# Four transposed-row loads, issued from ScalarE's queue instead of SyncE's, in a two-layer graph network kernel

## The chip, the cores and the metric

The kernel runs on one core of one Trainium2 chip. The metric is the time of one execution on the device in microseconds. Other times below are from one profiled execution; the profile counts them from the start of its span.

## What is computed

For each of 128 graphs of 128 nodes with 384 features, two layers of a directed graph network run, then a residual and a layer norm. The reference, cut to what matters:

```python
def layer(h, params):
    wl, b_l, ws, b_s, wr, b_r, g, beta = params
    u = jnp.einsum('bid,bjd->bij', h, h) / temper
    a = jax.nn.softmax(u, axis=-1)
    delta = a * adjacency_matrix
    attn = delta / (jnp.sum(delta, axis=-1, keepdims=True) + 1e-10)
    hl = h @ wl.T + b_l
    hs = h @ ws.T + b_s
    hr = h @ wr.T + b_r
    diag_a = jnp.diagonal(attn, axis1=1, axis2=2)
    ctx = (jnp.einsum('bij,bjd->bid', attn * upper, hl) + diag_a[..., None] * hs
           + jnp.einsum('bij,bjd->bid', attn * lower, hr))
    o = (ctx - mean) / jnp.sqrt(var + LN_EPS) * g + beta
    return (jax.nn.relu(o), None)
x = _layernorm(x + _L0_gnn_ref(x, adj, ...), axis=-1)
```

## The kernel before

One iteration `i` of a software pipeline works on several graphs at once: the projections of layer 1 for graph `i`, those of layer 2 for graph `i-3`, scores for graphs `i+1` (layer 1) and `i-2` (layer 2), the gathers (attention times projections) of graph `i-4` (layer 2) and `i` (layer 1). Layer 1 is `k = 0` in the code and layer 2 is `k = 1`. The function `run` issues the iterations: 0 to 7 written out, 8 to 123 in a hardware loop unrolled by four, and the rest, to 132, written out. Every engine has its own program with its instructions in an order written by hand, and semaphores join the programs. There is no planner.

Values are split into a rounded high part (ScalarE) and a low rest (GpSimd or VectorE), so that TensorE computes a product as three matmuls. TensorE's program is `project_and_score`, which interleaves 18 projection matmuls (L394) with three score steps (L388) and, after projection 14, one more score matmul that needs ScalarE's copy `cross` (L428), and `gather` (L458). The two layers share one set of accumulators `p_proj`, so a projection waits until VectorE has taken the former one out with its bias (`add_bias`, L562 and L566).

Two matrices are transposed through memory. The attention: VectorE transposes 32x32 blocks (L586), SyncE stores them (`store_attn`, L311) and loads them back block by block with four DMAs (`load_attn`, L328) into `attnT_whole`, which GpSimd cuts into its two sides (`cut_sides`, L816). The normalised rows of layer 1: ScalarE writes `normed` (L716), VectorE transposes its blocks (L596), SyncE stores them to `rows_mem` (`store_rows`, L333) and loads them back with four DMAs into `rowsT` (`load_rows`, L344). ScalarE then applies gain, shift and ReLU to `rowsT` in `relu_rows` (L733) in the iteration after the load and rounds the result (L739). `rowsT` has one buffer, so `load_rows` waits until `relu_rows` has read the graph before (`s_relu`), and until the store has landed (`s_rows_out`).

SyncE issues every DMA, in this order in an iteration: `xt_raw` (L355), the adjacency of layer 2 (L359), `store_rows`, `store_attn`, `xn` (L366), `load_rows`, `load_attn`, the adjacency of layer 1 (L373), `out` (L377). A store of the rows or of the attention waits for VectorE, and everything behind it in the queue waits with it.

ScalarE's order in an iteration is: `relu_rows(i-2)`, `cross_scores(0, i+1)` (L694), `high_sides(1)` (L707), the normalised rows (L716), `exponentials(0)` (L699), `high_sides(0)`, `high_projections(0)` (L712), `high_input` (L756), the squares (L744), the output rows (L716), `cross_scores(1, i-2)` (L694), `high_projections(1, i-3)` (L712), `exponentials(1, i-2)`. In iterations 0 and 1 the rounding of layer 2's weights (L760) ends the list.

Of the kernel before, what the change touches and what calls it, by code (L numbers as in the profile page):

```python
# [36 lines left out]
B = 32  # L37
# [15 lines left out]
def graph_block(nc: bass.Bass, xT: bass.AP, x: bass.AP, adj: bass.AP, WT: bass.AP, bias: bass.AP,  # L53
                gain_cols: bass.AP, shift_cols: bass.AP, gain_row: bass.AP, shift_row: bass.AP, out: bass.AP):
    G, N, D = x.shape
    C = D // P
# [6 lines left out]
    with ExitStack() as ctx:  # L63
        def sb(name, shape, dtype=F32):
            return ctx.enter_context(nc.sbuf_tensor(name, shape, dtype))
# [4 lines left out]
        def sem(name):  # L70
            return ctx.enter_context(nc.semaphore(name))
# [30 lines left out]
        rowsT = sb("rowsT", [P, C, N])  # L102
# [32 lines left out]
        rows_mem = [nc.dram_tensor(f"rows_mem_{slot}", (P, D), F32, kind="Internal").ap() for slot in range(2)]  # L135
# [16 lines left out]
        s_rows_out = [sem("s_rows_out_even"), sem("s_rows_out_odd")]  # L152
        s_rows_in = [sem("s_rows_in_even"), sem("s_rows_in_odd")]
# [43 lines left out]
        s_relu = sem("s_relu")  # L197
# [10 lines left out]
        def live(i, b):  # L208

            return not isinstance(i, int) or 0 <= b < G  # L210

        def done(eng, s, b):

            if not isinstance(b, int) or b >= 0:
                eng.wait_ge(s, b + 1)

        def moved(eng, pair, b, slot):

            if not isinstance(b, int) or b >= 0:
                eng.wait_ge(pair[slot], (b - slot) * 8 + 16)  # L220
# [11 lines left out]
        def direct_rows(i, b):  # L232

            return isinstance(i, int) and b == G - 1
# [40 lines left out]
        def col(tile, slot, k):  # L275
            return tile[:, slot, k:k + 1]
# [4 lines left out]
        def _(sp):  # L281
# [49 lines left out]
            def store_rows(b, slot):  # L331
                done(sp, s_rows_blocks, b)
                sp.dma_start(rows_mem[slot], rows_blocks[:]).then_inc(s_rows_out[slot], 16)  # L333

            def load_rows(b, slot):
                moves, read = (b - slot) * 8 + 16, b
                if not isinstance(b, int):
                    moves, read = sp.snap(moves), sp.snap(read)
                sp.wait_ge(s_rows_out[slot], moves)
                if not isinstance(b, int) or b >= 1:  # L340
                    sp.wait_ge(s_relu, read)
                blocks = rows_mem[slot].rearrange("(r a) (c s b) -> s a c r b", a=B, b=B, c=C)
                for s in range(4):
                    sp.dma_start(rowsT[s * B:(s + 1) * B, :, :].rearrange("a c (r b) -> a c r b", b=B),  # L344
                                 blocks[s]).then_inc(s_rows_in[slot], 16)

            done(sp, s_diag[0], 0)
            sp.dma_start(adj_tile[0][:, 0], adj[2]).then_inc(s_adj[0][0], 16)

            def iteration(i, p):  # L350
                q = 1 - p
                if live(i, i + 3):

                    done(sp, s_lo[0], i + 1)
                    sp.dma_start(xt_raw[:, q], xT[i + 3]).then_inc(s_xt[q], 16)  # L355
                if live(i, i - 1):

                    done(sp, s_attn[1], i - 3)
                    sp.dma_start(adj_tile[1][:, q], adj[i - 1]).then_inc(s_adj[1][q], 16)  # L359
                if live(i, i - 1) and not direct_rows(i, i - 1):  # L360
                    store_rows(i - 1, q)
                store_attn(i, p)
                if live(i, i - 3):

                    done(sp, s_y, i - 5)
                    sp.dma_start(xn[:, q], x[i - 3]).then_inc(s_xn[q], 16)  # L366
                if live(i, i - 1) and not direct_rows(i, i - 1):
                    load_rows(i - 1, q)
                load_attn(i, p)
                if live(i, i + 3):  # L370

                    done(sp, s_attn[0], i + 1)
                    sp.dma_start(adj_tile[0][:, q], adj[i + 3]).then_inc(s_adj[0][q], 16)  # L373
                if live(i, i - 5):

                    done(sp, s_o, i - 5)
                    sp.dma_start(out[i - 5], o[:, q]).then_inc(s_out[q], 16)  # L377

            run(sp, iteration)

            moved(sp, s_out, G - 2, 0)
# [308 lines left out]
        def _(act):  # L690
            def cross_scores(k, b):

                done(act, s_parts[k], b)
                nc.scalar.activation(cross[k][:], p_score[k][:, LO, :], ACT.Copy).then_inc(s_cross[k], 1)  # L694
# [20 lines left out]
            def normalise(which, rows_in, rows_out, s_rows):  # L715
                nc.scalar.activation(rows_out, rows_in, ACT.Identity, bias=nbias[:, which:which + 1],  # L716
                                     scale=rstd[:, which:which + 1]).then_inc(s_rows, 1)
# [23 lines left out]
            def squared_denominators(k, b, slot):  # L741
# [2 lines left out]
                nc.scalar.activation(eps_units[k][:, slot:slot + 1], col(rows[k], slot, EXPSUM), ACT.Square,  # L744
                                     bias=col(rows[k], slot, ADJSUM), scale=ATTN_EPS).then_inc(s_denom2[k], 1)

            def finish(i, q):
                moved(act, s_out, i - 7, q)
                done(act, s_y_nbias, i - 5)
                normalise(2, y[:], o[:, q, :], s_o)  # L750
# [19 lines left out]
            def iteration(i, p):  # L770
                q = 1 - p
                if isinstance(i, int) and i == 0:
                    high_input(1, 1)
                if live(i, i - 2):
                    relu_rows(i, i - 2, p)
                if live(i, i + 1):
                    cross_scores(0, i + 1)
                if live(i, i - 4):
                    high_sides(1, i - 4)
                if live(i, i - 1):  # L780
                    done(act, s_nbias, i - 1)
                    if not direct_rows(i, i - 1):

                        done(act, s_rows_blocks, i - 2)
                    normalise(0, gathered[:], normed[:], s_normed)
                if live(i, i + 1):
                    exponentials(0, i + 1, q)
                if live(i, i):
                    high_sides(0, i)
                    high_projections(0, i)  # L790
                if live(i, i + 2):
                    high_input(i + 2, p)
                if live(i, i + 1):
                    squared_denominators(0, i + 1, q)
                if live(i, i - 3):
                    squared_denominators(1, i - 3, q)
                if live(i, i - 5):
                    finish(i, q)
                if live(i, i - 2):
                    cross_scores(1, i - 2)  # L800
                if live(i, i - 3):
                    high_projections(1, i - 3)
                if live(i, i - 2):
                    exponentials(1, i - 2, p)
                if isinstance(i, int) and i == 0:
                    high_weights(1, UP)
                    high_weights(1, LOW)
                if isinstance(i, int) and i == 1:
                    high_weights(1, SELF)
# [118 lines left out]
```

## Time and profile before

| | before |
|---|---|
| median of 3 runs | 1686.35 us (1685.6 to 1686.82) |
| the profiled execution | 1685.81 us |
| its span in the profile | 1683.7 us |
| TensorE matmul busy | 1641.0 us (97%) |
| TensorE weight loads busy | 1590.4 us (94%) |
| VectorE busy | 1455.0 us (86%) |
| GpSimd busy | 1185.6 us (70%) |
| ScalarE busy | 933.2 us (55%) |
| share of 16 DMA engines | 42.5% |

The profiled execution lies 2.1 us over its span and 0.5 us under the median of the runs. Busy time counts no waits, no semaphore work and no issuing of DMAs; the rows of engine "SPq" are SyncE's queue and show how long an issue held it. A row of the timeline gives the start, the length, the engine, the line and the operation, and "x4" means that four like instructions were merged into it.

### The profile page before, as it was taken

Reading aid. Unit: us, or ns where it says so; the run is one execution under the profiler, and the core shown is the slowest. Engines: PE = TensorE matmul, PEld = TensorE weight load, DVE = VectorE, ACT = ScalarE, POOL = GpSimd, SP = SyncE. Lnnn points to the kernel's source line nnn. Section 1 sums busy time; section 2 is a strip of 40 time slices with the busy share of each in tenths; the row PEclk is TensorE's granted clock in tenths of the full one; section 3 lists DMA queues with packets and bytes.
Section 4 is the critical chain, followed back from the end, with each engine's and each line's share of the span. In section 5 each row is a group of like instructions: output and inputs, shape, how many; then the busy total and the mean of one; then the engine's idle time right before and its main releaser. Section 6 shows DMA issues by size and latency. Waiting matters only on the chain.

```text
span 1683.7 us, 35740 instructions
## 1 busy us (share of the span) xinstructions
PE 1641.0 (97%) x9478; PEld 1590.4 (94%) x9478; DVE 1455.0 (86%) x4625; ACT 933.2 (55%) x2438; POOL 1185.6 (70%) x1539
## 2 busy tenths in 40 slices
PE   6999999999999999999999999999999999999985
PEld 5999999999999999999999999999999999999985
DVE  6788888888888888888888888888888888888876
ACT  4555555555555555555655555555555555555552
POOL 3577777767767767767777777776776776777762
PEclk9999999999999999999999999999999999999997
DMA  5444444444444444444444444444444444444431
GB/s 183 93 110 107 108 108 107 110 106 107 113 104 111 112 104 110 112 104 111 109 107 109 110 108 108 105 112 107 107 113 104 111 111 104 110 112 105 107 84 36
DMA packets 471767, 180.88 MB, mean 107 GB/s; under 512 B 355776, under 2 KB 470720, under 8 KB 471744
## 3 DMA queue, kind: packets, MB, share of 16 engines
q1 hardware_dynamic: 471744, 180.61, 42.5%
q8 instruction: 9, 0.15, 0.0%
q14 instruction: 14, 0.11, 0.0%
HBM read 113.77 MB, written 66.72 MB: 107 GB/s over the span
## 4 chain that ended last, share of the span: by engine, by line
POOL 62%; issue 20%; DVE 8%; DMA 3%; ACT 3%; SPq 2%; PE 2%; POOLq 1%; DVEq 0%; ACTq 0%
POOL proj_split L252 24%; POOL rstd L825 11%; POOL attnT L816 10%; POOL attnT_split L821 10%; POOL hT_layer L850 5%; POOL nbias L829 3%; DVE proj L562 2%; ACT proj_split L712 2%; DMA rows_mem<-rows_blocks 1%; DVE p_gather L531 1%; SPq L344 1%; DVE y L537 1%; DVE stats L541 1%; PE p_proj L394 1%; DMA attnT_whole<-attn_mem 1%
## 5 line engine op out<-in xcount | busy, mean ns | idle before, releaser
L394 PE MATMUL p_proj<-w,hT_layer 128*128 128x384 f32 x6912 | 1397.8, 342 | 1.1 <-DVE proj L562 0.7
L394 PEld LDWEIGHTS p_proj<-w,hT_layer 128*128 128x128 f32 x6912 | 1168.8, 189 | 26.2 <-DVE proj L562 21.3
L252 POOL TENSOR_TENSOR proj_split<-proj,proj_split 128x768 fp32r<-128x768 f32 x252 | 465.6, 1848 | 409.3 <-ACT proj_split L712 409.2
L712 ACT ACTIVATE proj_split<-proj 128x768 fp32r<-128x768 f32 x256 | 214.8, 839 | 546.5 <-DVE proj L562 546.5
L458 PE MATMUL p_gather<-proj_split,attnT_split 128*128 128x384 f32 x1536 | 313.6, 339 | 21.2 <-POOL attnT_split L821 10.9
L458 PEld LDWEIGHTS p_gather<-proj_split,attnT_split 128*128 128x128 f32 x1536 | 272.8, 190 | 24.6 <-POOL attnT_split L821 18.1
L562 DVE TENSOR_TENSOR proj<-p_proj,bias_all 128x768 f32<-128x768 f32 x256 | 243.3, 950 | 5.6 <-PE p_proj L394 5.1
L825 POOL TENSOR_TENSOR rstd<-veps,neg_half 128x1 f32<-128x1 f32 x384 | 211.9, 552 | 33.9 <-DVE veps L510 15.0
L388 PE MATMUL p_score<-hT_layer 128*128 128x256 f32 x768 | 217.2, 284 | 8.1 <-POOL hT_layer L850 8.1
L821 POOL TENSOR_TENSOR attnT_split<-attnT,attnT_split 128x256 fp32r<-128x256 f32 x256 | 190.0, 742 | 14.5 <-ACT attnT_split L707 14.5
L816 POOL TENSOR_TENSOR attnT<-attnT_whole,sides 128x256 f32<-128x256 f32 x253 | 187.4, 741 | 5.9 <-DMA attnT_whole<-attn_mem 5.9
L707 ACT ACTIVATE attnT_split<-attnT 128x256 fp32r<-128x256 f32 x256 | 107.0, 418 | 101.0 <-POOL attnT L816 100.3
L733 ACT ACTIVATE p_rows<-rowsT,shift,gain 128x128 f32<-128x128 f32 x381 | 154.3, 444 | 9.6 <-DMA rowsT<-rows_mem 9.6
L388 PEld LDWEIGHTS p_score<-hT_layer 128*128 128x128 f32 x768 | 144.7, 189 | 8.7 <-issue 5.2
L566 DVE TENSOR_TENSOR proj<-p_proj,bias_all 128x384 f32<-128x384 f32 x256 | 141.5, 553 | 1.0 <-PE p_proj L394 1.0
L552 DVE TENSOR_TENSOR hT_layer<-p_rows,hT_layer 128x384 fp32r<-128x384 f32 x128 | 71.5, 558 | 77.0 <-ACT hT_layer L739 77.0
L850 POOL TENSOR_TENSOR hT_layer<-xt_raw,hT_layer 128x384 fp32r<-128x384 f32 x128 | 130.2, 1017 | 10.3 <-ACT hT_layer L756 10.3
L716 ACT ACTIVATE normed<-gathered,nbias,rstd 128x384 f32<-128x384 f32 x128 | 90.8, 709 | 45.4 <-POOL nbias L829 45.4
L531 DVE SCALAR_TENSOR_TENSOR p_gather<-p_gather,rstd,shift 128x384 f32<-128x384 f32 x128 | 80.2, 626 | 34.5 <-POOL rstd L825 33.9
L716 ACT ACTIVATE o<-y,nbias,rstd 128x384 f32<-128x384 f32 x128 | 88.9, 694 | 14.5 <-POOL nbias L829 14.5
L699 ACT ACTIVATE p_score<-scores,rows 128x128 f32<-128x128 f32 x256 | 90.4, 353 | 2.1 <-DVE rows L573 2.0
L586 DVE STREAM_TRANSPOSE attn_blocks<-attn 128x128 f32<-128x128 f32 x253 | 78.9, 312 | 8.8
(52 smaller groups left out, 1541.8 us busy)
## 6 DMA issues: line engine op xcount, KB each, us to landing
xt_raw<-xT SPq DMA_DIRECT2D x128, 192.0 KB, 2.6
xn<-x SPq DMA_DIRECT2D x128, 192.0 KB, 2.4
out<-o SPq DMA_DIRECT2D x128, 192.0 KB, 2.0
rows_mem<-rows_blocks SPq DMA_DIRECT2D x127, 192.0 KB, 1.9
rowsT<-rows_mem SPq DMA_DIRECT2D x508, 48.0 KB, 2.4
adj_layer<-adj SPq DMA_DIRECT2D x256, 64.0 KB, 1.9
attn_mem<-attn_blocks SPq DMA_DIRECT2D x124, 128.0 KB, 1.7
attnT_whole<-attn_mem SPq DMA_DIRECT2D x496, 32.0 KB, 2.2
```

Of the source, the lines that this page charges most:

```text
L252: op.tensor_tensor(proj_split[k][:, LO], proj[k][:, UP:LOW + 1, :], proj_split[k][:, HI].bitcast(F32), ALU.subtract).then_inc(s_proj_lo[k], 1)
L388: return nc.tensor.matmul(p_score[k][:, HI:LO + 1, :], hT[k][:, slot, HI, n, :], hT[k][:, slot, HI:LO + 1, n, :], start=(n == 0), stop=(n ...
L394: return nc.tensor.matmul(p_proj[:, which, 0:D], hT[k][:, slot, st, c, :], w[:, k, which, mv, c, :], start=(n == 0), stop=(n == 8))
L458: last = nc.tensor.matmul(p_gather[k][:, 0:D], AT_split[k][:, st, side, :], proj_split[k][:, mv, side, :], start=(side == UP and n == 0), ...
L562: nc.vector.tensor_tensor(proj[k][:, UP:LOW + 1, :], p_proj[:, UP:LOW + 1, 0:D], bias_all[:, k, UP:LOW + 1, :], ALU.add).then_inc(s_biased ...
L712: nc.scalar.activation(proj_split[k][:, HI], proj[k][:, UP:LOW + 1, :], ACT.Copy).then_inc(s_proj_hi[k], 1)
L716: nc.scalar.activation(rows_out, rows_in, ACT.Identity, bias=nbias[:, which:which + 1], scale=rstd[:, which:which + 1]).then_inc(s_rows, 1)
L733: last = nc.scalar.activation(relu_T[:, c, :], rows_in[:, c, :], ACT.Relu, bias=shift1[:, c:c + 1], scale=gain1[:, c:c + 1])
L816: nc.gpsimd.tensor_tensor(AT[k][:], AT_whole[:, k].unsqueeze(1).broadcast_to([P, 2, N]), sides[:], ALU.mult).then_inc(s_side[k], 1)
L821: nc.gpsimd.tensor_tensor(AT_split[k][:, LO], AT[k][:], AT_split[k][:, HI].bitcast(F32), ALU.subtract).then_inc(s_side_lo[k], 1)
L825: return nc.gpsimd.tensor_tensor(rstd[:, which:which + 1], veps[:, which:which + 1], neg_half[:], ALU.pow)
L850: nc.gpsimd.tensor_tensor(hT[0][:, slot, LO], xt_raw[:, slot], hT[0][:, slot, HI].bitcast(F32), ALU.subtract).then_inc(s_lo[0], 1)
```

## The change

`load_rows` leaves SyncE's program and enters ScalarE's, between `cross_scores(1, i-2)` and `high_projections(1, i-3)`. It keeps the wait for the store. The wait for `s_relu` goes, since `relu_rows` of the graph before stands earlier in the same program, and ScalarE has waited for it there. The four DMAs, their shapes and their semaphore are unchanged. In SyncE's program `load_attn` now follows the load of `xn`.

In the diff's context, `high_projections(1, i - 3)` is the rounding of the projections of `k = 1`, which this text calls layer 2.

```diff
-            def load_rows(b, slot):
-                moves, read = (b - slot) * 8 + 16, b
-                if not isinstance(b, int):
-                    moves, read = sp.snap(moves), sp.snap(read)
-                sp.wait_ge(s_rows_out[slot], moves)
-                if not isinstance(b, int) or b >= 1:
-                    sp.wait_ge(s_relu, read)
-                blocks = rows_mem[slot].rearrange("(r a) (c s b) -> s a c r b", a=B, b=B, c=C)
-                for s in range(4):
-                    sp.dma_start(rowsT[s * B:(s + 1) * B, :, :].rearrange("a c (r b) -> a c r b", b=B),
-                                 blocks[s]).then_inc(s_rows_in[slot], 16)
-
...
-                if live(i, i - 1) and not direct_rows(i, i - 1):
-                    load_rows(i - 1, q)
                 load_attn(i, p)
...
+            def load_rows(b, slot):
+
+
+                act.wait_ge(s_rows_out[slot], (b - slot) * 8 + 16)
+                blocks = rows_mem[slot].rearrange("(r a) (c s b) -> s a c r b", a=B, b=B, c=C)
+                for s in range(4):
+                    nc.scalar.dma_start(rowsT[s * B:(s + 1) * B, :, :].rearrange("a c (r b) -> a c r b", b=B),
+                                        blocks[s]).then_inc(s_rows_in[slot], 16)
+
...
                 if live(i, i - 2):
                     cross_scores(1, i - 2)
+                if live(i, i - 1) and not direct_rows(i, i - 1):
+                    load_rows(i - 1, q)
                 if live(i, i - 3):
                     high_projections(1, i - 3)
```

## Rows read from the trace of the kernel before

**Rows 1.** Windows: length, then busy PE, PEld, DVE, ACT, POOL, clock, DMA share, GB/s.
```profile
0.00:60.00 60.00, 42.55 (x214) 39.84 (x215) 36.23 (x104) 28.47 (x65) 21.77 (x35) 0.94 0.53 158
600.00:1300.00 700.00, 700.00 (x4082) 680.48 (x4081) 619.59 (x1984) 397.83 (x1047) 513.85 (x662) 1.00 0.43 109
1600.00:1683.70 83.70, 60.23 (x311) 57.16 (x309) 58.33 (x166) 31.44 (x75) 37.56 (x56) 0.85 0.23 60
```

**Rows 2.** Waits from 600 to 1300 us: total us, times, longest.
```profile
ACT proj_split L712 <- DVE proj L562: 238.5, 55, 4.3
...
PEld p_proj L394 <- DVE proj L562: 8.7, 41, 0.2
PEld p_score L428 <- ACT cross L694: 5.1, 28, 0.2
```

**Rows 3.** Timeline of one iteration, the compute rows around ScalarE's gap.
```profile
803.64 0.25 ACT L694 ACTIVATE cross<-p_score 128x128 fp32r<-128x128 f32 x1
...
805.64 0.56 DVE L537 SCALAR_TENSOR_TENSOR y<-p_gather,xn 128x384 f32<-128x384 f32 x1
...
807.25 0.95 DVE L562 TENSOR_TENSOR proj<-p_proj,bias_all 128x768 f32<-128x768 f32 x1
...
808.23 0.85 ACT L712 ACTIVATE proj_split<-proj 128x768 fp32r<-128x768 f32 x1 [4.33 <-DVE proj L562]
...
809.36 1.21 ACT L733 ACTIVATE p_rows<-rowsT,shift,gain 128x128 f32<-128x128 f32 x3
...
810.96 0.73 POOL L816 TENSOR_TENSOR attnT<-attnT_whole,sides 128x256 f32<-128x256 f32 x1
811.00 0.27 ACT L694 ACTIVATE cross<-p_score 128x128 fp32r<-128x128 f32 x1
...
811.32 0.19 PEld L428 LDWEIGHTS p_score<-ident_r,cross 128*128 128x128 f32 x1
```

**Rows 4.** Timeline of the same iteration, SyncE's queue.
```profile
801.35 0.33 SPq L333 DMA_DIRECT2D rows_mem<-rows_blocks  x1
801.89 0.32 SPq L311 DMA_DIRECT2D attn_mem<-attn_blocks  x1
802.40 0.34 SPq L366 DMA_DIRECT2D xn<-x  x1
803.25 2.58 SPq L344 DMA_DIRECT2D rowsT<-rows_mem  x4
806.02 2.52 SPq L328 DMA_DIRECT2D attnT_whole<-attn_mem  x4
```

**Rows 5.** Lines L344 and L328 over the span: length of an issue, time to landing.
```profile
L344 SPq DMA_DIRECT2D rowsT<-rows_mem x508: 563/618/695, 29.2 to 1631.6; - x170
...
DMA to landing us min/median/max: 2.2/2.4/3.1
...
L328 SPq DMA_DIRECT2D attnT_whole<-attn_mem x516: 318/612/923, 20.7 to 1642.7; - x172
...
DMA to landing us min/median/max: 1.7/2.2/3.9
```

**Rows 6.** Windows of two loads: length, clock, DMA share, GB/s.
```profile
803.20:805.80 2.60, 1.00 0.49 110
806.00:808.60 2.60, 1.00 0.39 61
```

**Rows 7.** Timeline of ScalarE in the first iterations.
```profile
28.24 1.15 ACT L760 ACTIVATE w<-w_raw 128x1152 fp32r<-128x1152 f32 x1
...
50.94 0.28 ACT L694 ACTIVATE cross<-p_score 128x128 fp32r<-128x128 f32 x1
54.43 0.85 ACT L712 ACTIVATE proj_split<-proj 128x768 fp32r<-128x768 f32 x1 [3.22 <-DVE proj L562]
```

**Rows 8.** Timeline of GpSimd and TensorE where they waited at the ends.
```profile
58.66 0.74 POOL L816 TENSOR_TENSOR attnT<-attnT_whole,sides 128x256 f32<-128x256 f32 x1 [1.46 <-DMA attnT_whole<-attn_mem]
...
1624.85 0.74 POOL L816 TENSOR_TENSOR attnT<-attnT_whole,sides 128x256 f32<-128x256 f32 x1 [0.65 <-DMA attnT_whole<-attn_mem]
...
1627.09 1.33 PE L458 MATMUL p_gather<-proj_split,attnT_split 128*128 128x384 f32 x6 [0.69 <-POOL attnT_split L821]
```

## The prediction

> **What bounds the kernel now.** I read the windows first. From 600 to 1300 us TensorE is busy for all of the 700 us, while ScalarE is busy for 398 of them and GpSimd for 514 [rows 1]. The stretches that hold TensorE's idle time are the first 60 us (17.5 us without a matmul) and the last 84 us (23.5 us) [rows 1]. So a change can gain time only at the two ends, and in the middle it can only lose, unless it makes TensorE itself quicker, which moving a DMA doesn't.
>
> Next the waits of the middle. ScalarE waits before its rounding of layer 2's projections (L712) 55 times for 238.5 us, which is 4.3 us in each iteration [rows 2]: this is the gap into which the four issues go. TensorE's weight loads wait a little for two engines, 0.2 us at most: for VectorE's bias addition, and 28 times in 55 iterations for ScalarE's copy of the cross scores [rows 2]. That second line is the warning in the profile. ScalarE's work from L712 to that copy is just in time for TensorE, so whatever delays ScalarE there delays TensorE nearly one for one.
>
> Last, one iteration in order of time. ScalarE ends its cross copy at 803.64 + 0.25 = 803.89 and starts L712 at 808.23, when VectorE's addition (807.25 + 0.95 = 808.20) is done. It goes on to the ReLU of the transposed rows at 809.36, to the cross copy at 811.00 (until 811.27), and TensorE loads that copy at 811.32 [rows 3]. SyncE issues the row loads at 803.25, as soon as the store of 801.35 has landed after 1.9 us, in 2.58 us, and the attention loads from 806.02 in 2.52 us [rows 4].
>
> **The change part by part.**
>
> *Four issues on ScalarE.* The trace has no DMA issued from ScalarE, so the price of one there is bounded by rows of SyncE's queue. The nearest is the same DMA: 618 ns median, 695 at most [rows 5]. The lower end is the 318 ns of a smaller load [rows 5]; the upper end is its 923 ns [rows 5]. I take 0.62, for it is the same shape, and with the small gaps between issues four take the 2.58 us of SyncE [rows 4]. They start at about 803.95, end at 806.5, and L712 may not start before 808.20 in any case. The cost is nil with 1.7 us to spare; at 923 ns each they end at 807.7, and still nothing is paid. The point at which ScalarE comes late to L712 is (808.2 - 803.95) / 4 = 1.06 us an issue. The wait that is carried along, for the store, is over at 803.25, before ScalarE gets there, so in the middle it holds up nobody. Queued behind it are L712, on which GpSimd waits, the exponentials and the ReLU.
>
> *The rows land later.* The first of four starts at 803.95 instead of 803.25, 0.7 us later. The last starts three steps of 0.65 on, at 805.9, and lands 2.4 us after its issue [rows 5], at 808.3. ScalarE reads the rows at 809.36 [rows 3]. That leaves 1.1 us where there were 1.8. With the longest landing of this load, 3.1 us [rows 5], it is 809.0, still in time. With a landing that doesn't change, this edge is reached when an issue takes (809.36 - 2.4 - 803.95) / 3 = 1.0 us, a little before the edge at L712. Each further 0.1 us an issue makes the ReLU, the cross copy and TensorE 0.3 us late.
>
> *SyncE loses 2.6 us of issues.* The attention loads come next in its queue. They wait for the attention's store, issued at 801.89; with the 1.9 us that the row store took it has landed at 803.8, so they start there and not at 806.02, 2.2 us earlier, and so does what follows in the queue until it meets its own waits. GpSimd reads the attention at 810.96 [rows 3], after its own work, and has no wait for it in the middle: no gain. The wait for the ReLU that goes was long over: no gain.
>
> *Both groups of loads are in flight together.* Windows of the same length show a DMA share of 0.49 while the rows (and the end of `xn`) are issued and 0.39 while the attention is [rows 6]. Their sum is 0.88, so 16 engines can carry both, but hardly with nothing lost. `xn` was issued at 802.40 [rows 4] and is read at 805.64 [rows 3]; it had the row loads behind it before, too. I take a few tenths of a microsecond in landing, which the 1.1 us hold. In the other direction, a landing of 3.9 us, the longest that the attention's loads show [rows 5], would end at 809.8, 0.44 us late.
>
> *The ends.* At the start, layer 2's weight rounding at 28.24 [rows 7] falls behind the row loads in the program, and these wait for the first store until 29.2, the first issue of the line [rows 5]. The rounding moves to about 32, and VectorE's part after it slips; GpSimd then waited for the attention in any case, so I book 0 to 0.2 us. In iteration 3 the cross copy ends at 51.22 and L712 starts at 54.43 [rows 7]; four issues after the store's landing at 51.7 end at 54.3: just hidden. Two places gain, for the attention lands earlier. At 58.66 GpSimd waited 1.46 us for it [rows 8]. TensorE was hardly idle there, and I book 0.3 of it. At 1624.85 GpSimd waited 0.65 us for it, and TensorE's gather at 1627.09 shows an idle 0.69 us just before it that GpSimd ended [rows 8]; the chain of work to the end of the kernel starts there, so I book 0.65.
>
> **Sum.** The middle 0, the start -0.3 + 0.1, the end -0.65: -0.85 us. Against the profiled execution, 1685.81 with its span of 1683.7, that is 1684.96 with a span of 1682.85. The median of the runs lies 0.54 above the profiled execution, so the forecast is 1685.5 us. With everything that the two waits at the ends could give (2.1 us) it is 1684.2, with none 1686.4. A measurement of this kernel can tell some 0.2% from no change, which is 3.4 us; the forecast is well inside.
>
> **Rivals.**
>
> *A, slower: the issues of two queues take turns.* If a queue can't issue while the other does, the eight issues stand in a row from 803.8, at 0.61 each. ScalarE's last one then starts at 803.8 + 7 x 0.61 = 808.1, ends at 808.7, which is 0.5 us late for L712, and lands at 810.5, which is 1.1 us late for the ReLU at 809.36 [rows 3]. The cross copy has no slack, so TensorE stops for 1.1 us in each of some 123 iterations of the full pipeline: 135 us, 1821 us in all. It decides when sharing stretches an issue beyond 1.0 us, from 0.62. For it: nothing in this trace shows two queues at once, so nothing excludes it. Against it: an issue of 32 KB and one of 48 KB take the same time (612 and 618 ns [rows 5]), which looks like work of the queue itself and less like something shared that grows with the transfer.
>
> The Trainium skill states the rule behind this rival (Perfetto Trace Analysis, "DMA Instruction — HWDGE (DVE, Sync)"): the block that generates descriptors is shared by the issuing sequencers and locked for exclusive use, with a lock wait counted into the issue. By that rule with the whole issue under the lock the time would be the 1821 us of this rival; no row shows how much of an issue it holds. Its page DMA: Bandwidth & Descriptors ("Issuing engines are not separate DMA queues") says that issuing from several engines saves only the sequencer's issue time; no row here shows that either, and by it the forecast stands.
>
> *B, slower: the rows land late.* The two groups of small packets share the engines from 803.95 to 808 and a landing takes 3.9 us: 0.44 us in 123 iterations is 54 us, 1740 us. For it: the shares add up to 0.88. Against it: landings of 2.4 us while `xn` was still moving. Between landings of 3.5 and 3.9 the price goes from 0 to that.
>
> *C, slower: an issue costs ScalarE more than 1.0 us.* At 1.1 us the loss is 0.3 us an iteration, 37 us, 1722 us; at 1.2 us it is 1759. For it: no row prices an issue there. Against it: every row of this shape lies between 0.56 and 0.70.
>
> *D, faster by over 0.2%.* It takes 3.4 us, and the waits for the attention that TensorE could feel sum to 2.1 us; the rest would have to come from a middle that is full. If the change did nothing at all (ScalarE issues no earlier and nobody waited for the attention), the time would be 1686.4, which can't be told from the forecast.
>
> **How the numbers follow.** Forecast 0.66 (1684 to 1688), A 0.12, B 0.10, C 0.08, D 0.04. Faster 0.04, same 0.66, slower 0.30. The range goes from 1682.5, just beyond the most that the ends can give, up to 1740, which takes in B and half of C; A, the rest of C and most of D stay outside, 0.2 together.
>
> **What would show it.** Right: four DMA rows on ScalarE's queue of some 0.6 us each, beginning at its cross copy's end; L712 still waiting for VectorE, about 1.7 us; no wait of the ReLU for `rowsT` beyond the first iterations; the attention loads starting 2.2 us earlier against the row store; 700 us of matmuls in 700 us; the two waits of GpSimd for the attention at the ends gone. Wrong: row-load issues of over 1.0 us (A if SyncE's attention loads stretch as well, C if they don't), ReLU waits of some tenths for the DMA with short issues (B), or TensorE's weight loads waiting long for the cross copy.

## The result, and the profile after

| | before | changed |
|---|---|---|
| median of 20 runs | 1687.37 us | 1684.1 us |
| lowest and highest | 1685.54 and 1688.73 | 1682.77 and 1687.42 |
| ratio, 95% interval | | 0.9984 [0.9977, 0.9991] |
| span of the profiled execution | 1683.7 us | 1680.8 us |

The changed kernel is 0.16% faster, some 3 us. That is clear of no change by its interval, less than the 0.2% that was called a change, and over three times the 0.85 us of the forecast. Measured again beside the variants it was 0.9983 [0.9974, 0.9992]. The before kernel's own medians were 1685.2 to 1687.4 us in the comparisons here and below, so ratios are compared, not times.

The windows of the changed kernel, with the columns of [rows 1]:

```profile
0.00:60.00 60.00, 41.86 (x208) 38.79 (x209) 34.85 (x97) 28.40 (x66) 21.95 (x36) 0.94 0.53 157
600.00:1300.00 700.00, 700.00 (x4079) 680.35 (x4078) 619.34 (x1983) 397.77 (x1045) 513.49 (x661) 1.00 0.43 108
```

The middle is as full as before, and its waits (total us, times, longest, from 600 to 1300 us) are those of [rows 2]:

```profile
ACT proj_split L698 <- DVE proj L548: 238.4, 55, 4.4
...
PEld p_proj L380 <- DVE proj L548: 8.7, 41, 0.2
PEld p_score L414 <- ACT cross L680: 6.8, 37, 0.2
```

ScalarE still waits 4.3 us for VectorE at the same place, with four issues inside the gap. The iteration of [rows 3, 4], in the changed kernel:

```profile
801.26 0.70 ACT L702 ACTIVATE o<-y,nbias,rstd 128x384 f32<-128x384 f32 x1
801.66 0.57 ACTq L739 DMA_DIRECT2D rowsT<-rows_mem  x1
801.86 0.26 ACT L680 ACTIVATE cross<-p_score 128x128 fp32r<-128x128 f32 x1
802.26 1.99 ACTq L739 DMA_DIRECT2D rowsT<-rows_mem  x3
806.44 0.85 ACT L698 ACTIVATE proj_split<-proj 128x768 fp32r<-128x768 f32 x1 [4.33 <-DVE proj L548]
...
807.58 1.22 ACT L719 ACTIVATE p_rows<-rowsT,shift,gain 128x128 f32<-128x128 f32 x3
```

```profile
800.08 0.33 SPq L311 DMA_DIRECT2D attn_mem<-attn_blocks  x1
800.59 0.34 SPq L354 DMA_DIRECT2D xn<-x  x1
801.81 2.73 SPq L328 DMA_DIRECT2D attnT_whole<-attn_mem  x4
```

"ACTq" is ScalarE's queue. The issues end at 804.25, 2.2 us before the rounding (L698). The attention loads start 1.7 us after their store where they started 4.1 us after it [rows 4]. GpSimd reads them at 809.16. The first issue begins before the cross copy that stands ahead of it in the program.

Issue length and landing (the time from the start of an issue until its data have arrived) over the span, as in [rows 5]:

```profile
L739 ACTq DMA_DIRECT2D rowsT<-rows_mem x508: 563/646/886, 29.4 to 1629.0; - x170
...
DMA to landing us min/median/max: 2.2/2.6/3.5
```

**Where the time came from.** The additions of VectorE (L562, after the change L548) follow the same graph in both traces, so their times can be subtracted. Four of them, before and after:

```profile
111.53 0.95 DVE L562 TENSOR_TENSOR proj<-p_proj,bias_all 128x768 f32<-128x768 f32 x1
...
159.66 0.95 DVE L562 TENSOR_TENSOR proj<-p_proj,bias_all 128x768 f32<-128x768 f32 x1
...
1594.40 0.95 DVE L562 TENSOR_TENSOR proj<-p_proj,bias_all 128x768 f32<-128x768 f32 x1
...
1660.47 0.96 DVE L562 TENSOR_TENSOR proj<-p_proj,bias_all 128x768 f32<-128x768 f32 x1 [0.39 <-PE p_score L428]
```

```profile
112.10 0.95 DVE L548 TENSOR_TENSOR proj<-p_proj,bias_all 128x768 f32<-128x768 f32 x1
...
157.46 0.95 DVE L548 TENSOR_TENSOR proj<-p_proj,bias_all 128x768 f32<-128x768 f32 x1
...
1593.13 0.95 DVE L548 TENSOR_TENSOR proj<-p_proj,bias_all 128x768 f32<-128x768 f32 x1
...
1657.59 0.96 DVE L548 TENSOR_TENSOR proj<-p_proj,bias_all 128x768 f32<-128x768 f32 x1 [0.28 <-PE p_score L414]
```

The differences are +0.57, -2.20, -1.27 and -2.88 us. So the start lost 0.6 us, the 48 us around the first trip of the hardware loop (a trip is four iterations, some 51 us) gained 2.8, the long middle gave 0.9 back, and the end gained 1.6. The prediction had nothing for the second stretch. There the kernel before had these waits (its waits of GpSimd for the attention that [rows 8] doesn't show):

```profile
84.45 0.74 POOL L816 TENSOR_TENSOR attnT<-attnT_whole,sides 128x256 f32<-128x256 f32 x1 [0.54 <-DMA attnT_whole<-attn_mem]
...
110.21 0.73 POOL L816 TENSOR_TENSOR attnT<-attnT_whole,sides 128x256 f32<-128x256 f32 x1 [0.33 <-DMA attnT_whole<-attn_mem]
...
136.76 0.74 POOL L816 TENSOR_TENSOR attnT<-attnT_whole,sides 128x256 f32<-128x256 f32 x1 [1.12 <-DMA attnT_whole<-attn_mem]
...
150.70 0.73 POOL L816 TENSOR_TENSOR attnT<-attnT_whole,sides 128x256 f32<-128x256 f32 x1 [1.21 <-DMA attnT_whole<-attn_mem]
...
1598.77 0.74 POOL L816 TENSOR_TENSOR attnT<-attnT_whole,sides 128x256 f32<-128x256 f32 x1 [0.61 <-DMA attnT_whole<-attn_mem]
```

With the two of [rows 8] they are seven, 5.9 us; the changed kernel has none. Taken addition by addition, the difference of the two traces falls by a step at each of the seven: 0.69, 0.56, 0.44, 1.04, 1.22, 0.80 and 0.70 us, in order of time, for waits of 1.46, 0.54, 0.33, 1.12, 1.21, 0.61 and 0.65. That is 5.4 us; some 2.6 of them are lost again, 1.3 before 60 us, 0.4 near 70 us and 0.9 over the middle.

The waits stand behind slow transfers. Before the wait at 136.76, SyncE's queue of the kernel before showed this:

```profile
125.97 0.33 SPq L333 DMA_DIRECT2D rows_mem<-rows_blocks  x1
126.51 0.32 SPq L311 DMA_DIRECT2D attn_mem<-attn_blocks  x1
127.02 1.58 SPq L366 DMA_DIRECT2D xn<-x  x1
129.62 0.58 SPq L344 DMA_DIRECT2D rowsT<-rows_mem  x1
```

The issue of `xn` took 1.58 us and not 0.34, the row store landed after 3.6 us and not 1.9, and with the row loads ahead of them the attention loads were late. From 120 to 165 us TensorE was busy for 43.43 us before and for 45.00 after.

**What stands beside the slow issues.** The page of the kernel before lists, apart from the queue of the kernel's own transfers, this queue of instructions (packets, MB, share of the 16 engines):

```profile
q8 instruction: 9, 0.15, 0.0%
```

Its nine packets have 16 KB each and start at 32.2, 59.6, 82.3, 100.8, 126.6, 148.6, 1589.3, 1615.2 and 1640.8 us. The six issues of SyncE that took over 0.95 us (the last stores of `out` left aside) start at 82.27, 101.12, 127.02, 148.64, 1589.40 and 1615.42: each has one of these packets beside it. In the fourteen kept traces there are 86 such issues, and 85 have a packet of q8 beside them; between 200 and 1550 us no trace has a packet of q8 or an issue over 0.86 us. So a transfer of instructions goes with each slow issue. That it is the cause is argued from this, for no experiment moved such a packet alone. It also tells why the changed kernel has no slow issue near 127 and 148 us: its packets start at 124.6 and 147.2, where SyncE, freed of four issues, had nothing to issue.

**The theory (S, slack).** The change gains nothing in an iteration that runs smoothly. It gives the attention loads 2.4 us of lead, and that lead swallows slow transfers, which occur mostly where the program enters and leaves the loop. In the first trip the two traces alone don't show the swallowing, since the changed kernel had no slow issue there; variants below do, with an issue of 1.2 to 1.3 us near 126 us, no wait of GpSimd for the attention and the same 2.7 to 2.8 us gained. The rivals: the gain comes from ScalarE's side (T), or from the written-out iterations alone (R). Beside this stands the theory of the gap (G): the cost is nil only because four issues fit between two edges, the rounding at L712 and the landing of the rows. Its rival (H) is that ScalarE with 45% idle time absorbs more.

### The profile page after: what moved, and what is told of

It is laid out like the page before. It is cut to its first block, busy times and chain, and to the rows that moved or that the text cites. A ratio compares the mean times of both kernels' runs of the same rounds, so it can differ in the third digit from the quotient of the medians.

```text
span 1680.8 us, 35643 instructions
## 1 busy us (share of the span) xinstructions
PE 1639.8 (98%) x9478; PEld 1590.7 (95%) x9478; DVE 1454.0 (87%) x4625; ACT 935.0 (56%) x2438; POOL 1186.6 (71%) x1539
## 4 chain that ended last, share of the span: by engine, by line
POOL 65%; issue 20%; DVE 8%; ACT 2%; PE 2%; DMA 2%; POOLq 1%; ACTq 0%; DVEq 0%; SPq 0%
POOL proj_split L252 25%; POOL rstd L822 11%; POOL attnT L813 10%; POOL attnT_split L818 10%; POOL hT_layer L847 5%; POOL nbias L826 3%; DVE proj L548 2%; ACT proj_split L698 2%; DVE p_gather L517 1%; DVE y L523 1%; DVE stats L527 1%; PE p_proj L380 1%; DMA rowsT<-rows_mem 1%; PE p_gather L444 1%; DMA rows_mem<-rows_blocks 1%
## 5 line engine op out<-in xcount | busy, mean ns | idle before, releaser
L698 ACT ACTIVATE proj_split<-proj 128x768 fp32r<-128x768 f32 x256 | 215.1, 840 | 546.2 <-DVE proj L548 546.1
L548 DVE TENSOR_TENSOR proj<-p_proj,bias_all 128x768 f32<-128x768 f32 x256 | 243.5, 951 | 5.3 <-PE p_proj L380 5.0
L702 ACT ACTIVATE normed<-gathered,nbias,rstd 128x384 f32<-128x384 f32 x128 | 91.0, 711 | 45.2 <-POOL nbias L826 45.2
L702 ACT ACTIVATE o<-y,nbias,rstd 128x384 f32<-128x384 f32 x128 | 89.3, 698 | 14.5 <-POOL nbias L826 14.5
```

What stands on the lines that cost most here:

```text
L548: nc.vector.tensor_tensor(proj[k][:, UP:LOW + 1, :], p_proj[:, UP:LOW + 1, 0:D], bias_all[:, k, UP:LOW + 1, :], ALU.add).then_inc(s_biased ...
L698: nc.scalar.activation(proj_split[k][:, HI], proj[k][:, UP:LOW + 1, :], ACT.Copy).then_inc(s_proj_hi[k], 1)
```

## The experiments

### ScalarE's part without SyncE's relief

SyncE gets four loads into a spare buffer where the row loads were:

```diff
+                if live(i, i - 1) and not direct_rows(i, i - 1):
+                    load_spare(i - 1, q)      # SyncE: 4 loads, rows_mem[slot] -> spare
                 load_attn(i, p)
```

> As the changed kernel, but SyncE issues four loads of the same shape, from the same rows into a spare buffer that nobody reads, at the place that the moved loads left. So ScalarE's part of the change is there and SyncE's relief is not; the reference's outputs are computed in full. Theory S: the attention loads are back at their old time, so the gain is gone and GpSimd waits for the attention again at the slow transfers, 1687.4 us or a little more (up to +3 us, for 1536 packets more are in flight in each iteration and the landing slack of the attention is about 0.75 us). Rival T (the gain comes from ScalarE's side, for example from the dropped wait for the ReLU): it stays at 0.9984. Rival A of the prediction (issues of two queues take turns): now eight issues of SyncE's queue and four of ScalarE's overlap, and issues of one queue stretch beyond 0.8 us.

Measured: 1689.56 us, ratio 1.0018 [1.0009, 1.0027]. The gain is gone and 0.2% on top. GpSimd waits for the attention eight times, 8.1 us in all: at the seven old places and once more at 74 us, the longest, 1.8 us, at 61. Four of them:

```profile
140.22 0.74 POOL L832 TENSOR_TENSOR attnT<-attnT_whole,sides 128x256 f32<-128x256 f32 x1 [1.16 <-DMA attnT_whole<-attn_mem]
...
153.63 0.74 POOL L832 TENSOR_TENSOR attnT<-attnT_whole,sides 128x256 f32<-128x256 f32 x1 [0.70 <-DMA attnT_whole<-attn_mem]
...
1602.15 0.73 POOL L832 TENSOR_TENSOR attnT<-attnT_whole,sides 128x256 f32<-128x256 f32 x1 [1.11 <-DMA attnT_whole<-attn_mem]
...
1628.91 0.74 POOL L832 TENSOR_TENSOR attnT<-attnT_whole,sides 128x256 f32<-128x256 f32 x1 [1.32 <-DMA attnT_whole<-attn_mem]
```

T falls: what counts is that SyncE issues less ahead of the attention. The 0.2% on top arose at the start, where the additions were 3.2 us later than before at 112 us; that the spare loads' own traffic has a part in it, or in the waits, isn't excluded by this run alone; the run with the other group on ScalarE, below, has no spare loads. The same trace settles rival A of the prediction. Two queues issue at the same time here:

```profile
806.13 2.59 SPq L349 DMA_DIRECT2D spare<-rows_mem  x4
...
806.29 0.56 ACTq L758 DMA_DIRECT2D rowsT<-rows_mem  x1
...
806.89 2.13 ACTq L758 DMA_DIRECT2D rowsT<-rows_mem  x3
```

Eight issues of the rows' shape take 2.9 us, from 806.13 to 809.02. One queue needs 2.58 us for four, so in turns they would have taken 5.2. Over the whole trace the median issue is 624 ns on SyncE's queue and 647 ns on ScalarE's, beside the 618 of one queue alone. The rule of the Trainium skill that the prediction cited against the change (Perfetto Trace Analysis, "DMA Instruction — HWDGE (DVE, Sync)", exclusive use of the generator) therefore costs next to nothing here: if a lock is held, it is for a small part of an issue. The sentence of DMA: Bandwidth & Descriptors ("Issuing engines are not separate DMA queues"), that a second issuer saves its sequencer time, agrees with this trace: 2.3 us saved of 5.2.

### The loop alone, and the rest alone

```diff
+        def by_scalar(i):
+            return not isinstance(i, int)      # loop_only; "isinstance(i, int)" in ends_only
...
-                if live(i, i - 1) and not direct_rows(i, i - 1):
+                if live(i, i - 1) and not direct_rows(i, i - 1) and by_scalar(i):
```

SyncE keeps the loads where ScalarE doesn't issue them.

> The row loads are issued from ScalarE in the hardware loop alone (iterations 8 to 123); in the iterations written out, at the start and at the end, SyncE issues them as before. Theory S (slack): the gain is the lead that the attention loads get in SyncE's queue; it is collected only where a transfer is slow, and the two places of the middle (GpSimd waits at 136.8 and 150.7 us of the kernel before, 1.1 and 1.2 us) lie in the first trips of the loop. Then this kernel has no wait of GpSimd for the attention between 120 and 1580 us, keeps those at 58.7 and in the last 90 us, and gains some 1.5 to 2 us (the 2.5 us less the drift of 0.7 us that the changed kernel showed over the middle): 0.9990, 1685.7 us. Rival R (the ends): the gain comes from the written-out iterations; then it is as the kernel before, 1687.4.

> The complement: ScalarE issues the row loads in the iterations written out, SyncE in the hardware loop. Theory S: the waits of GpSimd near 137 and 151 us stay where the transfers are slow, those at 58.7 and in the last 90 us go; gain some 1 us, 0.9994. The drift of the middle (VectorE's additions 0.006 us an iteration later against the kernel before) is nil. Rival R: the whole gain of the change, 0.9984.

Measured: 0.9988 [0.9979, 0.9997] and 0.9990 [0.9981, 0.9999]. Both parts gain, and their sum (0.22%) agrees with the whole (0.16%) within the intervals. R falls, for the loop alone gains too, though its interval only just leaves out 1. The waits go where ScalarE issues and stay where SyncE does. With ScalarE in the loop alone GpSimd has no wait between 112 and 1597 us and keeps five outside. With ScalarE at the ends alone only these two are left, in the first trip of the loop:

```profile
136.17 0.74 POOL L831 TENSOR_TENSOR attnT<-attnT_whole,sides 128x256 f32<-128x256 f32 x1 [0.63 <-DMA attnT_whole<-attn_mem]
...
149.28 0.74 POOL L831 TENSOR_TENSOR attnT<-attnT_whole,sides 128x256 f32<-128x256 f32 x1 [0.41 <-DMA attnT_whole<-attn_mem]
```

These two are half as long as in the kernel before (1.12 and 1.21), though SyncE issued there as before; the slow issues near 127 and 147 us took 0.97 and 1.06 us, not 1.58 and 1.29. So the additions of this trace gained 1.7 us in the first trip, where S had put nothing, and its profiled execution, the fastest of eleven, is as short as the changed kernel's. How the gain divides between loop and ends is thus less sure than that both have a part: a slow transfer costs more in one execution than in another.

The drift that I expected to follow the loads into the loop did not: counted by the additions as above, it was 0.1 to 0.2 us in both.

### The other group on ScalarE

```diff
-                load_attn(i, p)        # SyncE
...
+                load_attn(i, p)        # ScalarE, behind cross_scores(1, i - 2)
                 if live(i, i - 3):
                     high_projections(1, i - 3)
```

> The other group is moved: the four attention loads are issued from ScalarE, at the same place (behind the layer 2 cross copy), with their waits for the store and for GpSimd's cuts; the row loads stay on SyncE. Theory S: the attention loads start about 2 us earlier as in the changed kernel, and the rows keep their old time, so it gains as much, 0.9984, and perhaps the 0.7 us of drift as well. If the lead of the attention is not what counts, 1.000. The risk: ScalarE waits in its queue for the attention store to land, which in the start and the end may come late, and then layer 2's rounding is late; up to +2 us.

Measured: 0.9985 [0.9976, 0.9994], and no wait of GpSimd's cut for the attention. The gain is the same whichever group moves, as S has it, and no spare load is in play. The drift over the middle was 0.9 us here too, so the hope that it would go was wrong.

### Less slack for the attention, in the kernel before

```diff
                     load_rows(i - 1, q)
+                    load_spare(i - 1, q)      # 2 loads, rows_mem[slot] -> spare
```

> The kernel before, with two more loads of the rows' shape into a spare buffer in SyncE's queue between the row loads and the attention loads (the reference's outputs are computed in full). The attention loads start 1.3 us later. Theory S: in the kernel before they land some 0.75 us before GpSimd cuts them, so this is 0.5 us late in every iteration; TensorE feels 0.25 to 0.5 us of it, 30 to 60 us: 1717 to 1747 us, with GpSimd waiting for the attention over 100 times. If the attention loads had more slack than the timeline shows, 1687 to 1690.

Measured: 1743.06 us, 1.0336 [1.0316, 1.0355], 56.5 us more, or 0.46 us in each of 123 iterations. The waits from 600 to 1300 us:

```profile
PEld p_proj L408 <- DVE proj L576: 25.6, 54, 0.5
...
POOL attnT L830 <- DMA attnT_whole<-attn_mem: 20.0, 53, 0.7
```

GpSimd waits for the attention 53 times, once an iteration, for 0.38 us. So the kernel before had 1.3 less 0.4, some 0.9 us of slack there, near the 0.75 that I had read from the timeline. A slow transfer is longer than that, and so it reached TensorE.

### Both edges of ScalarE's gap

Four spare loads behind the row loads, then four ahead of them:

```diff
                     load_rows(i - 1, q)
+                    load_spare(i - 1, q)      # ScalarE: 4 loads; in eight_before it stands above
```

> As the changed kernel, but ScalarE issues eight loads: behind the four of the rows four more of the same shape into a spare buffer that nobody reads (the reference's outputs are computed in full). Theory G (the gap and its edges, as in the prediction): in the changed kernel the four issues run from 801.7 to 804.3 us and the rounding of layer 2's projections starts at 806.4; eight end at about 806.9, 0.5 us late, and all that ScalarE then does is 0.5 us late for TensorE in each of some 123 iterations: 55 to 65 us, about 1745 us. The rows themselves land as before, so the ReLU waits for nothing. Rival H (ScalarE's delay is absorbed, because it has 45% idle time): 1684 to 1690.

> The same eight issues with the four spare ones first, so that the row loads are issued 2.6 us later. Theory G: the last row load starts at about 806.3 and lands 2.6 us on, at 808.9, where the ReLU reads at 807.6: 1.3 us late in each of 123 iterations, 160 us, about 1845 us, with the ReLU waiting for the rows' DMA. So the edge of landing costs more than the edge at the rounding. Rival H: 1684 to 1690; if only ScalarE's queue counts and not the landing, as with the spare ones behind, 1745.

Measured: 1772.74 us (1.0512 [1.0492, 1.0532]) and 2059.33 us (1.2211 [1.2188, 1.2234]). H falls in both. With the spare loads behind, the whole is 0.70 us longer for each of 123 iterations, and an iteration of the middle takes 13.33 us and not 12.70, 0.63 longer, where I expected 0.5:

```profile
808.61 0.56 ACTq L752 DMA_DIRECT2D rowsT<-rows_mem  x1
808.82 0.25 ACT L682 ACTIVATE cross<-p_score 128x128 fp32r<-128x128 f32 x1
809.21 1.99 ACTq L752 DMA_DIRECT2D rowsT<-rows_mem  x3
811.31 2.63 ACTq L743 DMA_DIRECT2D spare<-rows_mem  x4
813.99 0.85 ACT L700 ACTIVATE proj_split<-proj 128x768 fp32r<-128x768 f32 x1 [4.92 <-DMA spare<-rows_mem]
```

ScalarE's idle time before L700 is 0.6 us more than the gap of 4.33: that much of the eight issues didn't fit, and it is what the iteration lost.

With the spare loads ahead I was wrong by more than a factor of two: 3.0 us an iteration and not 1.3. From 600 to 1300 us there are 45 iterations of 15.6 us, and these waits:

```profile
ACT proj_split L700 <- DMA spare<-rows_mem: 207.0, 39, 5.5
...
ACT p_rows L721 <- DMA rowsT<-rows_mem: 51.8, 45, 2.0
```

The ReLU's wait for the rows is 1.15 us, near what I expected, but it comes on top of the rounding's delay (5.3 - 4.3 = 1.0 us), which I had left out. The third part is the clock. TensorE waited 1.6 to 2.8 us for the cross copy in an iteration, and its granted clock fell:

```profile
612.00:618.00 6.00, 6.00 (x38) 5.94 (x37) 5.49 (x16) 1.23 (x3) 1.90 (x3) 1.00 0.69 140
618.00:624.00 6.00, 3.19 (x15) 2.86 (x14) 2.40 (x12) 3.59 (x10) 4.58 (x7) 0.87 0.15 35
624.00:630.00 6.00, 6.00 (x32) 6.00 (x31) 4.40 (x14) 2.66 (x7) 3.88 (x6) 0.85 0.40 106
```

Busy for 3.19 us of six, then full again, with a clock of 0.87 and 0.85: a part of each stretch ran at 1.2 GHz and the rest at 2.4. The mean over the 700 us is 0.94. TensorE's own account of these 700 us measures the clock apart from the waits: it was busy for 609.3 us, 13.6 an iteration where the kernel before took 12.7, and idle for 2.0 us an iteration. The 0.9 us are the clock's, the 2.0 those of the two waits (1.15 + 1.0 on ScalarE), and together they are the excess of 15.6 over 12.7.

### The lead without a second queue

```diff
-                if live(i, i - 1) and not direct_rows(i, i - 1):
-                    load_rows(i - 1, q)
                 load_attn(i, p)
+                if live(i, i - 1) and not direct_rows(i, i - 1):
+                    load_rows(i - 1, q)
```

> The kernel before with the two groups exchanged in SyncE's queue: attention loads first, row loads behind them, nothing on ScalarE. It gives the attention the lead without a second queue. Theory G: the last row load then starts at about 808.4 and lands at 810.8, where the ReLU reads at 809.4: 1.45 us late in each of some 123 iterations, at least 175 us, 1860 us, and more if TensorE's clock falls in the waits, as it did with the eight loads ahead (0.93). So the lead costs nothing only with a second queue. If the rows had the slack: 1684.

Measured: 1862.98 us, 1.1056 [1.1036, 1.1076]. From 600 to 1300 us the ReLU waits 49 times for the rows, 1.4 us each, the price expected, and an iteration takes 14.1 us and not 12.7:

```profile
ACT p_rows L733 <- DMA rowsT<-rows_mem: 68.7, 49, 1.8
```

So neither order of the two groups in one queue has slack for both: the rows had 1.8 us and the attention under 1, and a group of issues is 2.6 us long.

### The start: row loads on ScalarE from iteration 3 on, and weights rounded first

```diff
+        def by_scalar(i):
+            return not isinstance(i, int) or i >= 3      # from_three
```

> As the changed kernel, but SyncE issues the row loads of iterations 1 and 2, and ScalarE from iteration 3 on. In the changed kernel ScalarE stands in its queue in iterations 1 and 2 until the row store has landed, the rounding of layer 2's last weights waits 3.6 us behind it and VectorE's additions are 0.6 us late at 37 us of the trace and 1.3 us at 60. Theory: this delay goes and the rest of the gain stays, 0.5 us less than the changed kernel, 1683.6 us or 0.9981 of the kernel before; in the trace the additions near 37 us are back at the time of the kernel before. If the delay at the start is refilled later (TensorE's first full iterations absorb it), no difference to the changed kernel, 0.9984.

Measured: 1681.99 us, 0.9972 [0.9963, 0.9982]. But its trace didn't show the cause that I gave: the addition at 37 us was 0.7 us later than the changed kernel's, behind four row loads in SyncE's queue whose issues took 3.64 us. So it was run again, beside the changed kernel:

> The changed kernel once more, beside the variants below on the same chip, so that they can be compared with it and not only with the kernel before: 0.9984 of the kernel before. In its trace: are the slow transfers (issues of over 1 us, stores that take over 3 us to land) where they were, near 64, 101, 1588 and 1613 us? If they come from the program (its passage from the written-out code into the loop and out of it) they are at the same places; if they are chance they move.

> The kernel with SyncE's row loads in iterations 1 and 2 and ScalarE's from 3 on, again. It measured 0.9972 of the kernel before in another call, but its trace was as the changed kernel's from 100 us on and not earlier at 37 us, so the trace gives no reason for a gain over the changed kernel. If that is right: within 0.1% of changed_again. If the median was right: 0.1% faster, 1.5 to 2 us.

Measured on the same chip: 0.9983 [0.9974, 0.9992] for the changed kernel and 0.9971 [0.9959, 0.9982] for the one from iteration 3 on, medians of 1682.11 and 1680.19 us. Twice it is 0.12% better than the changed kernel; the intervals still overlap, so this is likely and not proved. In these two traces the addition of 111.53 us stood at 110.63 in the one and 112.76 in the other, 2.1 us apart, which would be the whole difference, but the first pair of traces has no such difference. The start varies by more than the effect.

The slow transfers came back at the same places in the repetition, near 64, 102, 1587 and 1612 us, which speaks against chance: all lie within some 50 us of the loop's two ends (near 105 and 1585 us), and each has its packet of q8 beside it. In both traces of the kernel from iteration 3 on there is another near 126 us (1.19 and 1.33 us), and GpSimd doesn't wait behind it: here the lead swallows a slow transfer.

```diff
-                if live(i, i - 1) and not direct_rows(i, i - 1):
+                if (live(i, i - 1) and not direct_rows(i, i - 1)
+                        and not (isinstance(i, int) and i == 1)):
                     load_rows(i - 1, q)
...
                 if isinstance(i, int) and i == 1:
                     high_weights(1, SELF)
+                    load_rows(0, q)
```

> As the changed kernel, but in iteration 1 ScalarE rounds layer 2's last weights before it enters the queue for the row loads, not behind them. In the changed kernel VectorE waited 2.35 us for that rounding and its addition at 37.4 us was 0.35 us later against the one before it than in the kernel before. Expected: VectorE's wait for the weights back below 1 us, the start some 0.4 us shorter, the time within 0.1% of changed_again (0.9982).

Measured: 0.9980 [0.9971, 0.9989], 1681.65 us beside 1682.11. VectorE's wait for the rounding of the weights in the first 60 us went from this (changed kernel, repeated)

```profile
DVE w L593 <- ACT w L755: 5.4, 3, 3.4
```

to this:

```profile
DVE w L593 <- ACT w L755: 1.3, 2, 0.9
```

The wait went as expected, and the 0.5 us can't be told from nothing.

## Why the prediction was right, and where it wasn't

**The middle costs nothing: right, for the reason given.** The four issues took 0.65 us each against the 0.62 taken from SyncE's rows, the rounding still waited 4.3 us for VectorE, the ReLU waited for the rows only in the first 110 us (five times), and TensorE was busy in 700 us of 700. The edges were right to 0.2 us, as the spare loads behind and the exchanged order show. The step from a delay to a time wasn't: with the spare loads ahead it left out the clock and the second wait.

**The start of the issues: wrong, on the safe side.** I let them begin when the cross copy ends. They began at 801.66, the copy ran from 801.86 to 802.12. ScalarE's queue issued the DMA while the engine was still at the output rows (L702) and the cross copy had yet to start. So the last row load starts at 803.6 and lands 2.6 us on, at 806.2, and 1.4 us are left to the ReLU, not 1.1.

**The landing: a little under.** 2.6 us where I took 2.4, 3.5 at most where the bound was 3.1. "A few tenths" was the right size, and rival B's 3.9 us did not occur.

**The ends: the term that was mis-sized.** I booked 0.3 and 0.65 us for two waits of GpSimd for the attention and said that the waits of this kind that TensorE could feel sum to 2.1 us. At these two the steps were 0.69 and 0.70, so the one at the end was priced right. But the kernel before has seven, 5.9 us. The two largest beside the one at 58.66 lie at 137 and 151 us, in the first trip of the loop, where I took the pipeline for full because a window from 600 us on was. The list of waits over the whole span had the total beside its count; I had priced two of its entries. The stretch around them gave 2.8 us, the end 1.6 where 0.65 was booked.

**The start of the kernel: under.** I booked a loss of 0 to 0.2 us for the weight rounding behind the queue and a gain of 0.3; measured was a net loss of 0.6 at 112 us, and 1.3 at 60 us, before the waits at 58.7, 84 and 110 us had paid. 0.2 of it was there at the first addition, before any row load. VectorE waited 2.35 us for the weights. The repetition was 1.2 us late at 112 us and 0.6 early at its first addition, so the start varies.

**The rivals.** A was tested by two queues issuing at once and fell. B and C did not occur. D, faster by over 0.2%, missed by little: the limit set for it, 2.1 us, was the mis-sized term. That 1684.1 us fell into the band of the forecast, 1684 to 1688, has luck in it: in that comparison the kernel before took 1687.37, 1.0 us more than the median that I forecast from, and 0.9984 of 1686.35 is 1683.7. The small gain was foreseen from the right kind of wait, but less than a third of its size; missed gains of 4.1 us by the steps stand against a loss at the start that was too small by over 1 us and the drift of 0.9.

**Still open.** Over the middle the changed kernel lost 0.9 us against the kernel before in its first trace. In its repetition it gained 1.1 us there; with the loads of the loop alone or the ends alone on ScalarE it lost 0.1 to 0.2. It comes evenly, 12.705 us an iteration against 12.697 before and 12.687 in the repetition. So it is no property of the change, and I have no cause. Nor was it tested that the instruction packets cause the slow issues, beside which they stand.

## What to carry to other kernels

A move that gains nothing in the smooth iteration can still pay by slack: ask which wait has the least of it, and list every place where a transfer is slow, the first trip of a loop and its exit above all, before the middle is called full and the ends are called the rest. A second issuing queue costs little when its engine waits for another at that point anyway, but only between two edges, the next instruction of that engine and the landing of what it issued; work out both before counting issues. When a group of waits is priced, start from the total over the span, and say which of its entries are booked.

## What the runs showed of the hardware

- Two queues issued at once almost at full rate: eight issues in 2.9 us, where one queue needed 2.58 us for four.
- ScalarE's queue issued a DMA at 801.66, 0.2 us before the activation ahead of it in the program had started (801.86), so its issues overlap its own computing.
- Around the passage into a hardware loop and out of it an issue of 0.34 us took 1.0 to 1.8 us, and a store landed after 3.6 us instead of 1.9. Of 86 issues over 0.95 us in the traces 85 had a 16 KB packet of the instruction queue q8 beside them; from 200 to 1550 us there was neither.
- With waits of TensorE for the cross copy of 1.6 to 2.8 us in an iteration of 15.6 us the granted clock was 0.94 on average from 600 to 1300 us; with idle times of 1.3 us in one of 14.1 us (the exchanged order) it was 1.00 there.
